# Turning normalised tiles on VectorE and through partition-to-partition transfers instead of on TensorE, in the projection stage of a transformer block

## The reference

```python
x = x + 0.5 * ffn(layernorm(x))
x = x + attention(layernorm(x))
x = x + 0.5 * ffn(layernorm(x))
```

## Time and profile before

| what | value |
|---|---|
| time, median of 3 runs | 1513.42 us (1511.14 to 1517.42) |
| the profiled execution | 1512.09 us, span 1510.3 us |
| busy share of the span | PE 98%, PEld 79%, DVE 63%, ACT 39%, POOL 46% |
| granted TensorE clock, mean | 0.999 of full speed |
| DMA, mean | 97 GB/s, 118725 packets |
| HBM | 95.72 MB read, 53.51 MB written |

### The profile page before, as it was taken

How to read it: one execution, slowest core, us unless ns; L and a number is a source line. 1 busy time by engine, 2 the same in 40 slices (tenths; PEclk the granted TensorE clock), 3 DMA queues, 4 the chain that set the end, 5 groups by cost and what they waited for, 6 DMA issues and landing times. The chain is left out here.

```text
span 1510.3 us, 25951 instructions
## 1 busy us (share of the span) xinstructions
PE 1483.6 (98%) x9216; PEld 1187.3 (79%) x9216; DVE 953.0 (63%) x2726; ACT 581.5 (39%) x1058; POOL 697.3 (46%) x384
## 2 busy tenths in 40 slices
PE   7999999999999999999999999999999999999999
PEld 7999999888888875555555555555489999999988
DVE  6645455655563858888998888888465343433433
ACT  4333332221211126666666666666542122221210
POOL 1332322443334438999999999999503010100100
PEclk9999999999999999999999999999999999999999
DMA  6323232542416162543333444330262112121201
GB/s 240 129 100 115 99 128 101 177 141 87 140 70 161 69 166 61 113 96 79 79 79 79 108 106 99 78 79 23 64 238 77 49 56 71 43 83 42 83 15 42
DMA packets 118725, 146.01 MB, mean 97 GB/s; under 512 B 40896, under 2 KB 77120, under 8 KB 118336
## 3 DMA queue, kind: packets, MB, share of 16 engines
q1 hardware_dynamic: 90304, 121.37, 28.0%
q10 hardware_dynamic: 28304, 23.14, 4.7%
HBM read 95.72 MB, written 53.51 MB: 99 GB/s over the span
## 5 line engine op out<-in xcount | busy, mean ns | idle before, releaser
L1698 ACT ACTIVATE at_probs<-ps 128x512 f32<-128x512 f32 (+1 forms) x640 | 314.9, 561 | 163.7 <-PE ps L1607 157.8
L69 DVE CUSTOM_DVE_ANT_0 ps<-ps,at_score_mask 128x512 f32<-128x512 f32 (+1 forms) x480 | 270.3, 622 | 23.5 <-PE ps L1596 21.8
L349 POOL TENSOR_TENSOR f_x_ring<-f_x_ring,f_half_bias 128x1024 f32<-128x1024 f32 x32 | 78.1, 2444 | 309.3 <-DVE f_h L638 303.1
L1539 POOL TENSOR_TENSOR at_added<-at_added,at_probs 128x2048 f32<-128x2048 f32 (+1 forms) x60 | 210.5, 3509 | 2.7 <-ACT at_probs L1698 0.9
L1624 PE MATMUL ps<-at_probs,at_vs 128*32 128x512 f32 (+3 forms) x1536 | 150.2, 494 | 0.3 <-POOL at_probs L1518 0.3
L75 PE MATMUL f_ps<-f_wt_hi,f_hT_hi 128*128 128x400 f32 (+1 forms) x384 | 133.4, 347 | 3.2 <-DVE f_hT_lo L642 3.2
L75 PE MATMUL ps<-f_wt_hi,f_hT_hi 128*128 128x400 f32 (+1 forms) x384 | 131.4, 342 | 0.0
L77 PE MATMUL f_ps<-f_wt_hi,f_hT_lo 128*128 128x400 f32 (+1 forms) x384 | 130.8, 341 | 0.0
L76 PE MATMUL f_ps<-f_wt_lo,f_hT_hi 128*128 128x400 f32 (+1 forms) x384 | 130.6, 340 | 0.0
L76 PE MATMUL ps<-f_wt_lo,f_hT_hi 128*128 128x400 f32 (+1 forms) x384 | 130.2, 339 | 0.0
L77 PE MATMUL ps<-f_wt_hi,f_hT_lo 128*128 128x400 f32 (+1 forms) x384 | 130.0, 338 | 0.0
(11 more groups left out here) (206 smaller groups left out, 3591.1 us busy)
## 6 DMA issues: line engine op xcount, KB each, us to landing
f_x_ring<-in_L_attn_resid SPq DMA_DIRECT2D x16, 512.0 KB, 3.5
x<-f_x_ring SPq DMA_DIRECT2D x16, 512.0 KB, 2.6
early<-x SPq DMA_DIRECT2D x16, 512.0 KB, 3.4
scr_q_hi<-qkv_rope_hi ACTq DMA_DIRECT2D x32, 256.0 KB, 2.0
scr_q_lo<-qkv_rope_lo ACTq DMA_DIRECT2D x32, 256.0 KB, 2.3
scr_ctx<-at_ctxn SPq DMA_DIRECT2D x32, 256.0 KB, 2.4
shared<-scr_ctx SPq DMA_DIRECT2D x16, 512.0 KB, 4.5
f_x_ring<-x SPq DMA_DIRECT2D x16, 512.0 KB, 3.7
```

The lines of the kernel that those rows point to most:

```text
L69: return dve.tensor_tensor_reduce(out=src[:, 0:keys], in0=src[:, 0:keys], in1=mask, scale=1.0, scalar=part_max[:, g, own] if c else -3.0e3 ...
L349: pool.tensor_tensor(x_ring[:, u, :], x_ring[:, u, :], half_bias[:], ALU.add).then_inc(bias_added, 1)
L1539: pool.tensor_tensor(added[:, heads, :], first, probs[:, (NU * n + u) % PROBS, heads, :], ALU.add).then_inc(added_done, 1)
L1698: act.activation(probs[:, (NU * n + u) % PROBS, g, cols], score_ps[x % BANKS][:, cols], ACT.Exp, scale=SCALE).then_inc(exp_done, 1)
```

## The change

For 12 of the 16 tiles (the four of the first chunk stay as they are) PE's `turn_h` goes away. In its place:

- DVE, in block o = 2j behind normalize, waits until all transfers of the tile before have landed (`landed`) and turns h in squares of 32x32 into `blocks`, the fourth tile of `early` (`to_blocks`: one transpose of 128x1024). Each square is turned in itself, but is still at its old place.
- SP, when that is done, issues 16 transfers (`turn`, `exchange`). Each takes 32 partitions with 8 runs of 32 elements (128 bytes) each and puts them on another (or the same) group of 32 partitions of hT_lo. 16 transfers of 32 KB make up the tile of 512 KB, in 4096 pieces of 128 bytes. They stand on SP's list ahead of the load of the tile after the next.
- ACT's high_hT and DVE's low_hT now read the turned tile from SBUF, where it has landed in the place of hT_lo, and low_hT works in place. Both stand two blocks later than before: for tile j in block 2j + 3.
- `normalize` no longer waits for PE to have read h.

The diff, with empty lines left out:

```diff
--- before.py
+++ after.py
@@ -47,6 +47,8 @@
 QH = NQ // 2
 KROWS = 3 * DH
 MASK = HALF + P
+SQ = 32
+EXCHANGED = (P // SQ) ** 2 * 16
 ROWS = [("row", i, g, c) for i in (*reversed(range(QH)), *range(QH, NQ)) for c in range(i // QH + 1) for g in range(G)]
 TURN_A, TURN_B = ("turn", 0), ("turn", 1)
 TURN_AT = QH * G + G
@@ -82,6 +84,15 @@
     eng.wait_ge(sem, value)
     eng.sem_inc(passed, 1)
+def exchange(sp, blocks, landing, loaded):
+    for a in range(P // SQ):
+        for b in range(P // SQ):
+            src = blocks[a * SQ:(a + 1) * SQ, :].rearrange("i (c b j) -> i c b j", b=P // SQ, j=SQ)[:, :, b, :]
+            sp.dma_start(landing[b * SQ:(b + 1) * SQ, :, a * SQ:(a + 1) * SQ].bitcast(F32), src).then_inc(loaded, 16)
 def ffn_weights(nc, ctx, name):
@@ -805,7 +816,7 @@
         wkv_lo = sb("wkv_lo", [P, KC, 2 * KV], F32R)
         wkv_raw = sb("wkv_raw", [P, WRAW, 2 * KV], F32)
         x_ring = early[:, 0:2, :]
-        h = early[:, 2, :]
+        h, blocks = early[:, 2, :], early[:, 3, :]
         stats = sb("stats", [P, 2, 6], F32)
         mv = sb("mv", [P, 2], F32)
         std = sb("std", [P, 1], F32)
@@ -848,6 +859,7 @@
         std_ready = sem("std_ready")
         h_ready = sem("h_ready")
         h_turned = sem("h_turned")
+        in_blocks = sem("in_blocks")
         hT_hi_done = sem("hT_hi_done")
         hT_lo_done = sem("hT_lo_done")
         proj_done = sem("proj_done")
@@ -878,6 +890,14 @@
             own = ROWS[(o - ROW_FROM) * PER_O:(o - ROW_FROM + 1) * PER_O] if ROW_FROM <= o < NO else []
             return [it for row in own for it in ([TURN_A, row] if row == ROWS[TURN_AT] else [row])]
+        def landed(t):
+            return TC + 1 + EXCHANGED * (t - TC + 1)
+        def tile_of(part, t):
+            return part[(t // TC) % NCH][:, :, (t % TC) * P:(t % TC + 1) * P]
         k_rows = scr["k_hi"].rearrange("n r t -> (n r) t"), scr["k_lo"].rearrange("n r t -> (n r) t")
         block = ctx.enter_context(nc.Block())
@@ -901,6 +921,13 @@
                 sp.wait_ge(h_ready, t + 1)
                 sp.dma_start(x_ring[:, slot, :], x_src[bass.ds(t * P, P), :]).then_inc(x_loaded[slot], 16)
+            def turn(t):
+                sp.wait_ge(in_blocks, t - TC + 1)
+                if t >= NCH * TC:
+                    sp.wait_ge(v_done, (t // TC - 1) * TC + 1)
+                exchange(sp, blocks, tile_of(hT_lo, t), h_turned)
             for loaded in x_loaded:
                 sp.sem_inc(loaded, 16 * TC // 2)
@@ -929,13 +956,17 @@
                     for slot in range(2):
                         load_x(TC + slot, slot)
                 if j in (WRAW + 2, WRAW + 4):
+                    turn(TC + j // 2 - 2)
                     load_x(TC + j // 2, j // 2 % 2)
                 if j >= WRAW:
                     sp.wait_ge(wkv_lo_done, j - WRAW + 1)
                 for cols, src in ((slice(0, KV), w["Wk"]), (slice(KV, 2 * KV), w["Wv"])):
                     sp.dma_start(wkv_raw[:, j % WRAW, cols], src[j * P:(j + 1) * P, :]).then_inc(wkv_loaded[j % WRAW], 16)
             for t in range(TC + 4, NT):
+                turn(t - 2)
                 load_x(t, t % 2)
+            for t in range(NT - 2, NT):
+                turn(t)
             sp.wait_ge(v_done, (B * NCH - 1) * TC + 1)
             for s in range(2):
                 sp.wait_ge(out_stored[s], NCH * NO * 16 + 16)
@@ -956,19 +987,13 @@
             pe.sem_inc(h_turned, 1)
             pe.sem_inc(v_done, 1)
-            def turn_h(b, t, first_tiles=False):
-                tile = b * (NCH * TC) + t
-                if not first_tiles:
-                    pe.wait_ge(h_ready, tile + 3)
-                    pe.wait_ge(hT_lo_done, tile + 1)
-                hT_ps = turned_ps[t if first_tiles else 0]
-                rows = early[:, t, :] if first_tiles else h
+            def turn_h(t):
                 for c in range(KC):
-                    last = pe.transpose(hT_ps[:, c, :], rows[:, c * P:(c + 1) * P], ident[:])
+                    last = pe.transpose(turned_ps[t][:, c, :], early[:, t, c * P:(c + 1) * P], ident[:])
                 last.then_inc(h_turned, 1)
             for t in range(TC):
-                turn_h(0, t, first_tiles=True)
+                turn_h(t)
             def by_pairs(outs):
@@ -1018,8 +1043,6 @@
                             if 1 <= c <= len(own):
                                 row_item(own[c - 1])
                         last.then_inc(proj_done, 1)
-                    if more and o % 2 == 1 and o // 2 < TC:
-                        turn_h(b, (ch + 1) * TC + o // 2)
                 for s in range(TC):
                     t = ch * TC + s
                     pe.wait_ge(v_copied, b * (NCH * TC) + (t + 1))
@@ -1047,9 +1070,12 @@
             def high_hT(b, t, early=False):
                 tile = b * (NCH * TC) + t
-                act.wait_ge(h_turned, tile + 2)
-                act.activation(hT_hi[(t // TC) % NCH][:, :, (t % TC) * P:(t % TC + 1) * P],
-                               turned_ps[t if early else 0], ACT.Copy).then_inc(hT_hi_done, 1)
+                if early:
+                    act.wait_ge(h_turned, tile + 2)
+                else:
+                    act.wait_ge(h_turned, landed(tile))
+                act.activation(tile_of(hT_hi, t), turned_ps[t] if early else tile_of(hT_lo, t).bitcast(F32),
+                               ACT.Copy).then_inc(hT_hi_done, 1)
             def high_out(b, g):
                 act.wait_ge(rope_done, b * (NCH * NO) + (g + 3))
@@ -1108,8 +1134,8 @@
                         high_out(b, g - 1)
                     if o >= 2:
                         store_out(b, g - 2)
-                    if more and o % 2 == 1 and o // 2 < TC:
-                        high_hT(b, (ch + 1) * TC + o // 2)
+                    if more and o % 2 == 1 and o > 1:
+                        high_hT(b, (ch + 1) * TC + o // 2 - 1)
                 if not more:
                     act.activation(std[:], eps[:], ACT.Exp)
@@ -1186,14 +1212,19 @@
                 dve.wait_ge(std_ready, tile + 1)
                 dve.reciprocal(rstd[:], std[:]).then_inc(ln_step, 1)
                 dve.wait_ge(ln_step, 4 * tile + 5)
-                dve.wait_ge(h_turned, tile + 1)
                 dve.tensor_scalar(h, x_ring[:, t % 2, :], mv[:, 0:1], rstd[:, 0:1], ALU.subtract, ALU.mult).then_inc(h_ready, 1)
+            def to_blocks(b, t):
+                tile = b * (NCH * TC) + t
+                dve.wait_ge(h_turned, landed(tile - 1))
+                wait_apart(dve, h_ready, tile + 3, passed)
+                dve.transpose(blocks, h).then_inc(in_blocks, 1)
             def low_hT(b, t, early=False):
-                hT_ps = turned_ps[t if early else 0]
-                hi, lo = [hT[(t // TC) % NCH][:, :, (t % TC) * P:(t % TC + 1) * P] for hT in (hT_hi, hT_lo)]
+                hi, lo = tile_of(hT_hi, t), tile_of(hT_lo, t)
                 dve.wait_ge(hT_hi_done, b * (NCH * TC) + (t + 1))
-                dve.tensor_tensor(lo, hT_ps, hi.bitcast(F32), ALU.subtract).then_inc(hT_lo_done, 1)
+                dve.tensor_tensor(lo, turned_ps[t] if early else lo.bitcast(F32), hi.bitcast(F32), ALU.subtract).then_inc(hT_lo_done, 1)
             def rope_sum(b, g):
                 dve.wait_ge(sin_done, b * (NCH * NO) + (g + 1))
@@ -1235,6 +1266,7 @@
                     if more and o % 2 == 0 and o // 2 < TC:
                         moments(b, (ch + 1) * TC + o // 2)
                         normalize(b, (ch + 1) * TC + o // 2)
+                        to_blocks(b, (ch + 1) * TC + o // 2)
                     dve.wait_ge(proj_done, b * (NCH * NO) + (g + 1))
                     wait_apart(dve, rope_done, b * (NCH * NO) + (g + 1), passed)
                     dve.stream_shuffle(rot[:, g % 2, :], bank, swap).then_inc(swapped, 1)
@@ -1242,8 +1274,8 @@
                     dve.tensor_tensor(rope[:, g % 2, :], bank, cos[:, cols], ALU.mult).then_inc(cos_done, 1)
                     if o >= 1:
                         rope_sum(b, g - 1)
-                    if more and o % 2 == 1 and o // 2 < TC:
-                        low_hT(b, (ch + 1) * TC + o // 2)
+                    if more and o % 2 == 1 and o > 1:
+                        low_hT(b, (ch + 1) * TC + o // 2 - 1)
                     if not more:
                         for it in items_of(o + 1):
                             row_item(it)
```

## The result

The changed kernel takes **1527.94 us** (median of 8 runs, 1525.18 to 1533.02) where the kernel before took 1517.38 (8 runs, the three of the table above among them): a ratio of **1.0091, 95% interval 1.0074 to 1.0107**. It is slower: by the ratio's interval 11 to 16 us. The profiled executions are 1525.92 against 1512.09, 13.8 us apart, with spans of 1524.2 and 1510.3. That pair is taken apart here.

A forecast was written before the change was run, and what follows sets the result against it. PE's own instructions were taken to bound the projection stage. -10.6 for transposes and +4.3 + 3.4 + 3.4 for value-copy waits gave +0.5 on 1512.1, then 1513.9 by the median, rounded to 1514 us; range 1503 to 1530.

The forecast's parts named there:

- The gain, -10.6: PE in the projection stage: 12 tiles no longer turned, 0.89 us each, -10.6 us.
- DVE's loop, 13.9: DVE from one low_hT to that two blocks later: 12.55 us grows to 13.9 with a transpose of 1.25; bounds 13.6 to 14.6.
- PE's waits for the value copy, 3.4 + 4.3 + 3.4: PE at value tile 2 waits for ACT's first value copy, 4.3 us in the second chunk, 3.4 in first and third.
- Both cost 0: Token-tile load moved back 7.5 us and first-chunk weight loads behind the transfers: wanted late enough to cost 0.
- 16 x 0.47 for the issues: SP's queue: 16 issues at 0.47 us plus 2.4 for landing, 9.9 us a tile, leaving 2.7 us spare.
- the third rival: The exchange sets DVE's pace, from an issue of 0.64 us; at 0.77, 19 us more, 1533; chance 0.17.
- The sum: Transposes and value-copy waits over three chunks: -10.6 + 4.3 + 3.4 + 3.4 = +0.5 us.
- the sign for which I gave 0.26: Whole kernel: slower by over 0.5%, chance 0.26; within 0.60, faster 0.14.
- The forecast's own bounds: Total time for a DVE loop of 13.6 to 14.6: -3 to +6, given as 1509 to 1521 us.
- The whole gain: Rival: DVE's transpose slips into its loop's waits or ACT's list gets through earlier; -10.6, 1503 us; chance 0.15.
- ACT's list gets through earlier: One way, within the rival of 1503 us and chance 0.15, for the full -10.6 to arrive.
- The meeting of low_hT with POOL: Rival: low_hT contends with POOL in SBUF, 12 times up to 0.75 us; +8, 1522; chance 0.10.

The follow-up runs named there:

- run 9: Run 8 with both first value copies ahead of high_out of block 7 and high_hT ahead of high_out in its block; 1503.72 us, ratio 0.9927.
- run 2: The kernel before, plus one DVE transpose of 128x1024 behind each of 12 normalize, result unused, no transfers; 1524.9 us, ratio 1.0049.
- run 6: The changed kernel with SP issuing the load of a token tile ahead of the 16 transfers; 1529.09 us, ratio 1.0088.
- run 7: Run 6 with one transfer of 128 partitions by 4 KB for the 16, leaving out the exchange between partition groups; 1525.97 us, ratio 1.0064.
- run 1: The changed kernel with the first two value copies and their stores ahead of high_out of block 8 in ACT's list; 1518.14 us, ratio 1.0019.
- run 3: The changed kernel without DVE's transpose in squares, the 16 transfers reading h itself; 1521.63 us, one execution.
- run 12: The changed kernel with ACT's list alone edited: both value copies ahead of high_out of block 7, high_hT ahead of high_out; 1507.05 us, ratio 0.9951.
- run 4: The changed kernel with 4 transfers of 32 partitions in 512-byte runs for the 16, leaving out the exchange between groups; 1537.1 us, one execution.
- run 8: The changed kernel, token load first, value copies 0 and 1 ahead of high_out of blocks 7 and 8, Wkv weights awaited piece by piece; 1518.49 us, ratio 1.0015.
- run 5: The changed kernel with 40 PE transposes of the identity ahead of its wait for value tile 2; 1527.68 us, ratio 1.0074.
- run 10: Run 9 with the buffer of squares doubled, each tile normalised in place and turned into one of two; 1506.15 us, ratio 0.9934.

## Why the prediction was wrong

- **The gain, -10.6: right** (12 x 0.89 is 10.7). 3.7, 3.6 and, in run 9, 3.5 to 3.7 a chunk.
- **DVE's loop, 13.9: right for what is added, a little short in the changed kernel.** With the transpose alone (run 2) it is 13.96; in the changed kernel 14.04 to 14.54, the longest with a store wait of ACT in it. The transpose took the 1.25 that I chose, low_hT from SBUF 1.23. (The step from normalize to the next start, 0.81 + 0.12 + 1.17, is 2.10 and not 2.04, which leaves the loop at 13.9.)
- **PE's waits for the value copy, 3.4 + 4.3 + 3.4: right in kind and place, too small in size.** They were 4.84, 5.07 and 4.33 in order of the chunks (3.4, 4.3 and 3.4 forecast), 14.2 for 11.1. In the first, the token load had met ACT's stores, and 1.6 of the wait is gone with the load first (run 6). In the second, the two loops ahead of the copy took 14.54 + 14.04, 0.8 more than twice 13.9, which is its whole excess; in the third 14.29 + 14.15, 0.6 of an excess of 0.9. The exchange is not the reason: run 7 has 13.4 without it.
- **No term for the clock: the step that failed.** I counted a wait of PE at its own length. In the changed kernel each of the four is followed by work at the lower clock: 8.5 us in all, of the 13.6 that the sum was off. The earlier trace rows have 1.00 all through because there is no wait in them; a row at 1.00 doesn't say what a new wait would do. The Trainium skill (TensorE: Matmul & The Clock Gate, Part 1: The HAM clock gate) says that an idle TensorE falls to 1.2 GHz and that sustained work brings 2.4 back; the trace agrees (0.50 behind the wait that ended at 338.68). It does not follow every wait of this length: those of 3.06 (run 1) and 3.01 (run 3) left the clock at 1.00, while 0.50 came behind one of 2.14 (run 3).
- **"Both cost 0", of the loads of weights and token tiles: failed.** The weights loaded behind the transfers, with DVE's longer loop too, made PE wait 3.0, and 4.9 with the clock. Runs 3 (no transpose) and 7 (no exchange) show that it needs both, and in run 12, with ACT's list put right, 2.5 of it is still there. The token load met ACT's stores (runs 4 and 6): ACT's waits for stores are 12.0 us up to 535 us where they were 4.4, and 5.3 of the 7.6 more are gone with the load first. PE saw about 1.6 of it.
- **16 x 0.47 for the issues: mis-sized.** 0.66 each (the last lands 1.9 behind its issue, for 2.4), just past the 0.64 at which I had the third rival decide. It did show: one wait of 2.3 of a transpose for a transfer, and 22.9 us of them in run 9, where low_hT no longer waits for ACT. It decides nothing, since the last link to PE is ACT's list and not DVE's pace. A threshold on one engine's loop is no threshold on the time.
- **The sum** was +0.5 where +14 came: +8.5 clock, +3.0 weights, +3.1 value waits, less 0.9 for the last chunk and the transposes (10.8 for 10.6). The range ended at 1530 and holds the result, but the sign for which I gave 0.26 came, and mostly by terms that neither the sum nor a rival had. (The forecast's own bounds, -3 to +6 about 1514, are 1511 to 1520, not 1509 to 1521.)
- **Rivals.** The whole gain did not arrive by itself; it did arrive in run 9, and all but the weights' part of it when ACT's list alone was put right (run 12). That list I had named ("ACT's list gets through earlier") without weighing it as a remedy. The meeting of low_hT with POOL did not happen in the changed kernel (1.23 each time but once, 1.38). In run 9 it did twice (2.31 and 2.32), as low_hT comes earlier there. DVE:

```profile
296.09 2.31 DVE L1238 TENSOR_TENSOR qkv_hT<-qkv_hT 128x1024 fp32r<-128x1024 f32 x1
...
324.48 1.21 DVE L1238 TENSOR_TENSOR qkv_hT<-qkv_hT 128x1024 fp32r<-128x1024 f32 x1
```

And POOL, beside the first of them:

```profile
295.57 1.75 POOL L1191 TENSOR_TENSOR qkv_rot<-qkv_rot,qkv_sin 128x512 f32<-128x512 f32 x1
```

That is 1.1 us more, where my bound was 0.75. low_hT starts 0.52 behind POOL's product and ends 1.08 behind its end (298.40, 297.32). The Trainium skill (SBUF — State Buffer, Who interferes with whom) has an instruction of VectorE with two SBUF inputs contend with one of GpSimd that reads SBUF; these rows agree.

## What to carry to other kernels

Work taken off the bounding engine makes it arrive sooner at every hand-over, so look up what each hand-over has in reserve (here 1 us at one copy) before counting the gain; the remedy may be the place of two instructions in another engine's list. Price a new wait of TensorE at its length, and name the work behind it at the lower clock as a term of its own: 1.6 to 2.9 us behind each of the four waits here, nothing behind two others of 3 us. When a queue gets a long run of new issues, follow the large load behind it: what matters is whose store it meets, and a shorter run can make that worse.

## What the hardware showed that I had not expected

- A wait of PE of 3 to 5 us cost another 1.6 to 2.9 in the changed kernel: the values parts grew by 6.9, 8.0 and 5.9 for waits of 4.84, 5.07 and 4.33. Of the waits of 2.1 to 3.1 us in the other profiles, two (3.06 in run 1, 3.01 in run 3) left the granted clock at 1.00, and 2.14 (run 3), 2.22 and 2.58 (run 8), 2.48 (run 12), 2.67 (run 1) and 2.77 (run 6) were followed by 0.50.
- Transfers of 32 partitions in pieces of 128 bytes took 0.61 of SP's queue each (585 to 1703 ns) and followed each other by 0.66; one of 128 partitions by 4 KB also took 0.60, while a weight load took 0.43.
- The time from the first values matmul of the last chunk to the end of the span came in two groups: 965.3 to 965.8 in six profiles, the kernel before, the changed one and run 9 among them, and 967.2 to 970.5 in eight others, runs 5 and 10 among them. In all eight of the longer ones, and in none of the six, the granted clock fell to 0.50 some 2 to 4.5 us behind a gap of 0.9 at the start of the attention, where PE has the same instructions and the same gap in all fourteen. So the same gap halves the clock in one execution and not in another, and 3 us of a difference between two single profiles of this kernel can be that alone. What decides it stays open. The first stage spreads as well: the projection stage begins between 261.0 and 266.5 us.
